# Graph attention with a sort by blocks: smaller first groups, a wide last one, a denser sort plan, and a reordered prologue

## What is computed

```python
q = (x[src] @ qW).reshape(e, 4, 24)
k = (x[dst] @ kW).reshape(e, 4, 24)
v = (x[dst] @ vW).reshape(e, 4, 24)
s = exp(clip(sum(q * k, -1), -10, 10))
w = s / (segment_sum(s, src)[src] + 1e-08)
res = segment_sum(w[:, :, None] * v, src).reshape(6250, 96)
out = layernorm(x + x + res)
```

## Time and profile before

| | us |
|---|---|
| median of 3 runs (lowest, highest) | 1357.38 (1355.97, 1362.27) |
| the profiled execution's own time | 1364.9 |
| its span, first to last instruction | 1363.1 |
| PE busy, share of the span | 1050.7 (77%) |
| DVE busy | 1019.2 (75%) |
| POOL busy | 957.1 (70%) |
| ACT busy | 674.0 (49%) |
| mean granted clock of PE | 0.709 |

### The profile page before, as it was taken

One profiled execution on the slowest core, in us unless ns is written; L12 is line 12 of the kernel. 1 busy time (PEld: TensorE's weight loads), 2 busy tenths in 40 slices (PEclk: granted clock), 3 DMA queues, 4 the chain that ended last, 5 costly groups with the idle time before them and its releaser, 6 DMA issues.

```text
span 1363.1 us, 23400 instructions
## 1 busy us (share of the span) xinstructions
PE 1050.7 (77%) x6502; PEld 935.0 (69%) x6503; DVE 1019.2 (75%) x2846; ACT 674.0 (49%) x1464; POOL 957.1 (70%) x911
## 2 busy tenths in 40 slices
PE   6896498776798786798887778887678888888850
PEld 4674497665787665698776667777577777777740
DVE  8797998689997678998758887777655555555556
ACT  4773299522599522399842225886232222222215
POOL 1203777777787777777777777777777777777745
PEclk9897599956699856599877555889665555555555
DMA  4300222222222222222222222222422222222212
GB/s 121 121 0 25 68 70 70 73 79 70 68 67 69 76 70 73 70 72 72 70 74 79 77 72 74 70 72 82 135 79 78 78 78 78 78 79 78 77 41 71
DMA packets 68298, 100.62 MB, mean 74 GB/s; under 512 B 33522, under 2 KB 53874, under 8 KB 68204
## 3 DMA queue, kind: packets, MB, share of 16 engines
q0 software_dynamic: 42240, 86.56, 23.3%
q1 hardware_dynamic: 25964, 12.94, 3.3%
HBM read 92.23 MB, written 7.22 MB: 73 GB/s over the span
## 4 chain that ended last, share of the span: by engine, by line
POOL 39%; DVE 18%; issue 16%; PE 14%; ACT 7%; DMA 4%; DVEq 2%; POOLq 0%; ACTq 0%; SPq 0%
POOL kv L466 39%; ACT steps_m L672 4%; PE ps_r L620 3%; DMA kv<-kv_table,dst_s 2%; DVE acc L1031 2%; PE ps_q L608 2%; DVE steps_m L800 2%; DVE prod L1039 2%; PE ps_a L594 1%; DVEq L392 1%; PE ps_b L594 1%; DMA acc<-in_x_dram 1%; DVE place_m L940 1%; DVE place_m L944 1%; ACT onehT L717 1%
## 5 line engine op out<-in xcount | busy, mean ns | idle before, releaser
L466 POOL DMA_INDIRECT kv<-kv_table,dst_s x880 | 921.9, 1048 | 329.5 <-issue 322.8
L620 PE MATMUL ps_r<-wv,oneh 128*128 128x100 f32 x1760 | 344.9, 366 | 127.4 <-DVE wv L1046 126.3
L620 PEld LDWEIGHTS ps_r<-wv,oneh 128*128 128x128 f32 x1760 | 312.5, 270 | 150.2 <-DVE wv L1046 141.1
L608 PE MATMUL ps_q<-qt,onehT 128*128 x1760 | 327.3, 353 | 90.9 <-ACT onehT L717 85.9
L608 PEld LDWEIGHTS ps_q<-qt,onehT 128*128 128x128 f32 x1760 | 298.3, 259 | 119.7 <-issue 118.6
L672 ACT ACTIVATE steps_m<-iota_f,pos_t 125x283 f16<-125x283 f32 (+4 forms) x778 | 321.3, 502 | 22.1 <-PE ps_b L594 13.9
L1031 DVE TENSOR_TENSOR acc<-acc,ps_r 128x100 f32 x880 | 223.2, 254 | 65.6 <-issue 32.4
L1039 DVE TENSOR_TENSOR prod<-ps_q,kv 128x480 f32<-128x480 f32 x176 | 115.3, 655 | 208.9 <-DMA kv<-kv_table,dst_s 201.2
L710 ACT ACTIVATE wv<-clipped 128x20 f32<-128x20 f32 x176 | 38.2, 217 | 433.1 <-DVE clipped L1073 432.9
L594 PE MATMUL ps_a<-steps_m,place_m 125*128 125x283 f16 (+4 forms) x778 | 197.8, 294 | 1.7 <-ACT steps_m L672 0.2
L717 ACT ACTIVATE onehT<-ps_t 128x640 f32<-128x640 bf16 x176 | 123.4, 701 | 148.6 <-PE ps_t L629 143.9
(11 more groups left out here) (185 smaller groups left out, 696.4 us busy)
## 6 DMA issues: line engine op xcount, KB each, us to landing
kv<-kv_table,dst_s POOLq DMA_INDIRECT x880
kv_table<-kv SPq DMA_DIRECT2D x7, 672.0 KB, 3.6
acc<-in_x_dram SPq DMA_DIRECT2D x6, 336.0 KB, 4.6
steps_m<-in_x_dram SPq DMA_DIRECT2D x6, 336.0 KB, 5.3
out_dram<-kv SPq DMA_DIRECT2D x6, 336.0 KB
src_i<-in_src_dram SPq DMA_DIRECT2D x1, 415.0 KB
dst_i<-in_dst_dram SPq DMA_DIRECT2D x1, 415.0 KB
acc<-in_x_dram SPq DMA_DIRECT2D x1, 288.0 KB, 5.7
```

The costliest lines, as they stand in the source:

```text
L466: nc.gpsimd.indirect_dma_start(kv[:, nm, u, :], None, kv_dram, bass.IndirectOffsetOnAxis(ap=dst_s[:, n * U + u:n * U + u + 1], axis=0)).th ...
L608: last = nc.tensor.matmul(ps_q[nm % 2][:, u * D:(u + 1) * D], onehT[:, nm % 2, u * P:(u + 1) * P], qt[:, bass.ds(blks[u], 1), :].rearrange ...
L620: last = nc.tensor.matmul(ps_r[nm % 2][:, u * RW:(u + 1) * RW], oneh[:, nm % 2, u, :], wv[:, nm % 2, u, :], start=True, stop=True)
```

## The change

The groups become `[140, 110, 140, 190, 270]` columns, so that `B0 = 0, 17, 39, 66, 103`, still 176 iterations in all, and the steps are 186, 205, 234, 283 and 361 columns wide. The plan of a group now gives its rank steps a computed share of the iterations and spreads the units over the others, up to two in an iteration; one iteration stands ahead of `differ` and `turn` together and one ahead of `pick`, and the first list is written three iterations ahead in place of four. For groups 1 to 4 this makes 7, 9, 11 and 15 rank iterations and 7, 10, 14 and 20 sort iterations. The loops of the main part are written out but for the last stretch. In the prologue `src` comes in two loads, group 0's columns first; x has four buffers in place of two; the first transposes (`lift`) stand behind the marks, projection 0 behind the tally, and the projections 3 to 6 behind `table`. ACT writes the three wide ramps `iota_s`, `iota_d` and `iota_t` in place of DVE, and POOL writes `times_f` and `plus_f`.

```diff
-    LS = 4
+    LS = (3, 4, 4, 4)
     Y = 6
 
-    GC = [180, 150, 170, 190, 160]
+    GC = [140, 110, 140, 190, 270]
...
-    def plan_iters(m, count):
-
-        end = m + count
-        looped = min(max(m, R), end)
-        reps = max(0, min(end, NBT - L) - looped) // R
-        PLAN.append(("iters", m, 0, [None] * (looped - m)))
-        PLAN.append(("loop", looped, reps, 0, 0, (0,) * R))
-        PLAN.append(("iters", looped + reps * R, 0, [None] * (end - looped - reps * R)))
-        return end
-
-    def plan_woven(m, g):
-
-        v, end = V0[g], V0[g + 1]
-        n = max(2, R - m)
-        PLAN.append(("iters", m, g, list(range(v, min(v + n, end + 1)))))
-        m, v = m + min(n, end + 1 - v), v + min(n, end + 1 - v)
-        reps = max(0, end - v) // R
-        PLAN.append(("loop", m, reps, g, v, (1,) * R))
-        m, v = m + reps * R, v + reps * R
-        PLAN.append(("iters", m, g, list(range(v, end + 1))))
-        return m + end + 1 - v
+    def plan_iters(m, count, units=()):
+
+        units = list(units) + [()] * (count - len(units))
+        PLAN.append(("iters", m, 0, units))
+        return m + count
+
+    def plan_last(m):
+
+        looped = max(m, R)
+        PLAN.append(("iters", m, 0, [()] * (looped - m)))
+        reps = max(0, NBT - L - looped) // R
+        PLAN.append(("loop", looped, reps))
+        PLAN.append(("iters", looped + reps * R, 0, [()] * (NBT + 2 - looped - reps * R)))
+
+    def shares(count, parts):
+
+        return [count * k // parts for k in range(parts + 1)]
...
-        project_after = {"mark0": (0,), "count": (1,), "base0": (2, 3), "sel0": (4,), "table": (5, 6)}
+        project_after = {"mark3": ("lift",), f"tally{len(ROUNDS[0]) - 1}": (0,), "count": (1,), "base1": (2,),
+                         "table": (3, 4, 5, 6)}
         for name in rank(0):
             PLAN.append(("piece", name, 0))
             for i in project_after.get(name, ()):
-                PLAN.append(("piece", "project", i))
+                PLAN.append(("piece", "lift", 0) if i == "lift" else ("piece", "project", i))
...
-        for g in range(G - 1):
-
-            end = B0[g + 1] - LS
-            spare = end - 3 - (V0[g + 2] - V0[g + 1] + 1) - m
-            assert spare > 2
-            names = rank(g + 1) + ["choose"]
-            at = 0
-            for k in range(spare):
+        for g in range(1, G):
+
+            end = B0[g] - LS[g - 1]
+            count = end - m - 2
+            names = rank(g) + ["choose"]
+            units = V0[g + 1] - V0[g] + 1
+            ranked = round(count * (12 * GC[g] + 1000) / (34 * GC[g] + 1000))
+            at = shares(len(names), ranked)
+            for k in range(ranked):
                 m = plan_iters(m, 1)
-                to = len(names) * (k + 1) // spare
-                for name in names[at:to]:
-                    PLAN.append(("piece", name, g + 1))
-                at = to
-            m = plan_woven(m, g + 1)
-            for name in ("differ", "turn", "pick"):
-                m = plan_iters(m, 1)
-                PLAN.append(("piece", name, g + 1))
+                for name in names[at[k]:at[k + 1]]:
+                    PLAN.append(("piece", name, g))
+            at = shares(units, count - ranked)
+            PLAN.append(("iters", m, g, [tuple(range(V0[g] + a, V0[g] + b)) for a, b in zip(at, at[1:])]))
+            m = plan_iters(m + count - ranked, 1)
+            PLAN.append(("piece", "differ", g))
+            PLAN.append(("piece", "turn", g))
+            m = plan_iters(m, 1)
+            PLAN.append(("piece", "pick", g))
             assert m == end
-        plan_iters(m, NBT + 2 - m)
+        plan_last(m)
...
-        xc = acc_m[:, 0:2 * CH].rearrange("p (i b d) -> p i b d", i=2, d=D)
+        xc = acc_m[:, 0:4 * CH].rearrange("p (i b d) -> p i b d", i=4, d=D)
...
-            sp.dma_start(src_i[:, :], src.rearrange("(p c) -> p c", c=EC)).then_inc(s_src, 16)
+            src_rows = src.rearrange("(p c) -> p c", c=EC)
+            sp.dma_start(src_i[:, 0:GC[0]], src_rows[:, 0:GC[0]]).then_inc(s_src[0], 16)
             load_x(0, xc[:, 0], s_x[0])
             for i, w in enumerate((qW, kW, vW)):
                 sp.dma_start(w_all[:, i * D:(i + 1) * D], w).then_inc(s_w, 16)
             load_x(1, xc[:, 1], s_x[1])
+            sp.dma_start(src_i[:, GC[0]:EC], src_rows[:, GC[0]:EC]).then_inc(s_src[1], 16)
             sp.dma_start(dst_i[:, :], dst.rearrange("(p c) -> p c", c=EC)).then_inc(s_dst, 16)
 
+            for i in (2, 3):
+                load_x(i, xc[:, i], s_x[i])
...
-                if i + 2 < NPC:
+                if i + 4 < NPC:
                     sp.wait_ge(s_xt, 2 * i + 2)
-                    load_x(i + 2, xc[:, i % 2], s_x[i % 2])
+                    load_x(i + 4, xc[:, i % 4], s_x[i % 4])
...
+            for k, (a, b) in enumerate(((P * 8 - 1, 0), (-P * 8, 1), (-P * 8, 0), (P * 8, 0))):
+                nc.gpsimd.memset(times_f[:, k:k + 1], float(a))
+                last = nc.gpsimd.memset(plus_f[:, k:k + 1], float(b))
+            last.then_inc(s_times, 1)
...
-                if sorts:
-                    unit(*sorts)
+                for sort in sorts:
+                    unit(*sort)
...
+            act.wait_ge(s_ramp, 1)
+            nc.scalar.activation(iota_s[:, :, :], iota_f[:, 0:P].unsqueeze(2).to_broadcast([P, P, SU]), ACT.Copy)
+            nc.scalar.activation(iota_d, iota_f[:, 0:T1].unsqueeze(2).to_broadcast([P, T1, KD]), ACT.Copy)
+            nc.scalar.activation(iota_t[:, :, :], iota_f[:, 1:P + 1].unsqueeze(2).to_broadcast([P, P, U]),
+                                 ACT.Copy).then_inc(s_wide, 1)
...
-            nc.vector.tensor_copy(iota_f[:, :], iota_i[:, :])
+            nc.vector.tensor_copy(iota_f[:, :], iota_i[:, :]).then_inc(s_ramp, 1)
             nc.vector.tensor_copy(iota_u[:, :], iota_i[:, 0:NB])
             link(nc.vector.tensor_copy(part_f[:, :], part_i[:, :]))
-            nc.vector.tensor_copy(iota_t[:, :, :], iota_f[:, 1:P + 1].unsqueeze(2).to_broadcast([P, P, U]))
...
-            link(nc.vector.tensor_copy(iota_s[:, :, :],
-                                       iota_f[:, 0:P].unsqueeze(2).to_broadcast([P, P, SU])))
...
-            link(nc.vector.tensor_copy(iota_d, iota_f[:, 0:T1].unsqueeze(2).to_broadcast([P, T1, KD])))
```

More of the change, by code:

```diff
@@ L271, in gnn @@
         ps_p = ps_r + ps_t
-        s_x = [sem("s_x0"), sem("s_x1")]
+        s_x = [sem(f"s_x{i}") for i in range(4)]
         s_xe = [sem(f"s_xe{i}") for i in range(NPC)]
@@ L280, in gnn @@
         s_w = sem("s_w")
-        s_src = sem("s_src")
+        s_src = [sem("s_src0"), sem("s_src1")]
         s_dst = sem("s_dst")
@@ L284, in gnn @@
         s_const = sem("s_const")
+        s_ramp = sem("s_ramp")
+        s_wide = sem("s_wide")
+        s_times = sem("s_times")
         s_xpad = sem("s_xpad")
@@ L705, in tiles @@
                 if sorts:
-                    unit(*sorts, halves=(0,))
+                    unit(*sorts[0], halves=(0,))
                 n, nm = m, mm
@@ L725, in tiles @@
                 if sorts:
-                    unit(*sorts, halves=(1,))
-            follow(act, tiles, unit, {"project": project, "differ": differ, "turn": turn,
-                                      **{f"tally{r}": lambda g, r=r: tally(g, r) for r in range(len(ROUNDS[G - 1]))}})
+                    unit(*sorts[0], halves=(1,))
+                for sort in sorts[1:]:
+                    unit(*sort)
+            follow(act, tiles, unit, {"lift": copy_xt, "project": project, "differ": differ, "turn": turn,
+                                      **{f"tally{r}": lambda g, r=r: tally(g, r) for r in range(max(len(r) for r in ROUNDS))}})
             act.wait_ge(s_wv, NBT)
@@ L966, in unit @@
             def unit(g, v, vm, between=lambda i: None):
+                if isinstance(v, int) and v == 0:
+                    dve.wait_ge(s_wide, 1)
                 wait(dve, s_bin, v - 1)
@@ L1076, in tiles @@
                 if sorts:
-                    unit(*sorts, between=lambda i: add_up(3 + i))
+                    unit(*sorts[0], between=lambda i: add_up(3 + i))
+                    for sort in sorts[1:]:
+                        unit(*sort)
                 else:
```

40 lines of the change are left out of this document (15 added, 25 removed).

## The result

The changed kernel takes **1406.21 us** (median of 4 runs, 1402.32 to 1407.84) where the kernel before took 1357.62 beside it (4 runs, 1355.97 to 1362.27): 1.034 times as long, 95% interval 1.031 to 1.037. The forecast was 1362 with a range to 1378, so the time lies 44 us above the forecast and outside the range. The profiled execution of the changed kernel took 1402.3 us, with a span of 1400.5.

The account below looks back on a forecast made before the run. POOL's gathers were taken to set the pace. After the change, 97 us to first gather, 759 for four lists, 459 for the last group's gathers and 53 finish gave 1368 us of span, converted to 1362 us; range 1338 to 1378.

Parts of the forecast that it names:

- Ranking: Rank stages of groups 1 to 4, bound by DVE: 39.8 us for 170 columns, 0.11 per column, 3.7 per iteration.
- the term of 759 us: Time for ranking, sorting and closing groups 1 to 4 in turn, against POOL's own 734; fourth list 25 us late.
- Part 2: The gathers: whether the four later groups' lists are ready when POOL, at 6.25 us an iteration, needs them.
- Close of a group: Last sort unit to written list, two iterations lying partly beside its waits: 14 us, 17 for the widest group.
- rival A: The sorters keep up, lists take 734 to 745 us, so time is 1337 to 1348; chance 0.28.
- Start of a sort: Allowance between ranking and sorting in each of groups 1 to 4: 2 us.
- the factor 0.9945: Conversion from profiled run to median time, from the kernel before: 1364.9 profiled, 1357.4 median.
- A wait in one place: POOL idles once, 13 to 37 us, near 830 to 856, for the fourth list; chance 0.59.
- B: PE at low clock bounds group 4's ranking, lists take 774 us, time 1377; chance 0.10.
- C: POOL and DVE hold each other up during gathers, surplus may double, POOL's own 826 us, time 1429; chance 0.03.
- D: Prologue gains less, say dst lands at 16; every case moves up by 3 us; no chance given.
- The break-even: Fourth list must come 754 us after the first gather for no net change; forecast 759.

Follow-up runs that it names:

- The set in between: Changed kernel with groups of 160, 140, 160, 190 and 200 columns, each list four iterations ahead: 1357.06 us, ratio 0.999 to the kernel before.
- control: The changed kernel with nothing edited, run on the chips where the kernel before takes about 1591 us: 1622.48 us, ratio 1.022.

## Why the prediction was wrong

**What held.** The first gather came at 97.91 (forecast 97), PE's first unit at 49.92 (49.6). The rows of the changed kernel:

```profile
14.73 0.23 DVE L812 TENSOR_SCALAR src_i<-src_i 125x140 int32<-125x140 int32 x1 [4.44 <-DMA dst_i<-in_dst_dram]
...
49.92 0.34 PE L597 MATMUL ps_a<-onehT,place_m 125*128 125x186 f16 x1 [2.63 <-ACT steps_m L679]
```

Waiting for `dst` came as said and 1.5 us worse (14.73 for 13.2), and the rest of the prologue made up for it. The tail after the last group's start took 459.4 us (459) and the finish 54.2 (53). Ranking took 305.9 (310.5) and ACT's rate in the sorts was met: 385.8 us busy in the four for 381.6 forecast, 1%. Sum: 97.9 + 789.0 + 459.4 + 54.2 = 1400.5. Three of the four terms are right to 2 us; one is 30 short. That ranking came out so near hides two slips in the working. By its own prices (39.8 for 170 columns, 0.11 a column, 3.7 an iteration) group 1 comes to 51.7 and group 4 to 106.3, where 49.5 and 108.5 stand; they cancel in the sum, and the right ones are nearer to the 51.0 and 105.5 measured.

**What failed** is the term of 759 us: the time of the four lists in Part 2, and in it two prices.

*Close of a group*, forecast 14, 14, 14 and 17, measured 17.8 to 21.5: 78 us for 59, **19 of the 30**. The prediction took the 7.7 us of a close with no iteration inside and let two iterations lie "partly beside its waits". They lie ahead of them. All engines follow one written order, so ACT's copy of the sums and PE's `pick` each queue behind a whole iteration: 4.0 and 4.9 us in the rows of group 1's close, 4 to 5 us for the third iteration in the experiment. 7.7 + 2 × 5 is 17.7, and group 1 measured 17.8. The values of rival A, closes of 11 and 13 us, went the wrong way, and the upper bounds, 17 and for the widest group 20, were under every one measured. The closes that the kernel before has between its iterations, three iterations in each and paced by POOL, lasted 28 to 31 us; the prediction set its price from the one close without iterations and did not bound it by these.

*Start of a sort*, forecast 2 us each: the sorts as a whole took 405.2 for 389.6, 16 over. ACT was idle for 19.5 us in them where the forecast had 8, and 12.9 of these are the two waits at each start, as in the rows at 697.96 to 705.05. The other 4 are the 1% of its busy time. Ranking gave 5 back.

*From span to time.* Of the 44 us, 32.5 are span. The rest is the factor 0.9945: it took the 7.5 us by which one profiled run of before lay above the median of its three runs for a property of the kernel, and the profiled run of after lay 3.9 below its own. Both are differences between single runs.

**A wait in one place** was the wrong picture too, and the prediction had named the waits at groups 1 and 2 as the sign that its stage rates are wrong. The first three lists were judged just in time from margins of 5, 7 and −2 us; stage sums that are 4 to 8% short make each of them late. That did not add to the end, since the chain of lists hardly waits for POOL (4.5 us with a third fewer buffers), but it is why 17 waits for buffers and three for lists came before the fourth list. POOL's own need was over-estimated by 25 us (789.0 less some 80 of waits is 709, forecast 734), without effect, as it was not the longer chain.

**The rivals.** A (the sorters keep up) needed 734 to 746 and got 789. B (PE at the low clock in the big ranking) fell by its own condition: the clock was 0.50 from 610 to 615, where the first tally starts, and 0.99 and 1.00 from 615 to 625, where the second and third run; the ranking took 105.5 us for 108.5. C (the port): the gathers' busy time would have doubled its surplus; it fell by 17.7 us. The Trainium skill, "SBUF — State Buffer", section "SBUF: two separate sides", has the port pair of VectorE and GpSimd as an exclusive lock, for VectorE instructions in a two-port mode or with two SBUF inputs against a GpSimd one that reads SBUF. Longer gathers in the sorts are there in the trace, but mild: 0.13 to 0.26 us over 0.95 each in the four sorts, 0.01 after the last list, and 904.2 us busy in all against 921.9. D: `dst` was late, by a part of its price.

**The range** was too narrow for its sum. The break-even was 5 us away, and 759 was a sum of sixteen stage estimates. 4% on it is 30 us, and the closes' upper bounds alone would have reached only 12.

## What to carry to other kernels

A chain that is hidden by a small margin is priced by its own length, and its short serial steps count most: in a kernel whose engines all follow one written order, each iteration placed ahead of a dependent step costs the chain that iteration's whole time, here 4 to 5 us in the close, whatever idles beside it. Widening the last group so that the prologue gets shorter moves the due time of the last list forward by far more (22 iterations, 137 us of gathers) than the start is gained by (23.5 us). The set in between kept two thirds of that gain, 15.5 us, and had its lists all but in time, yet came out even with the kernel before.

## What the hardware showed that was not expected

Two chips ran the kernel before some 230 us slower than the others, and the rows say why in part. On the first kind of chip the changed kernel's tenth gather ends at 110.4, and DVE takes the second iteration's rows at 112.21. On the second kind, control with six buffers, then eight (each time the last gather before POOL stops for a buffer, the next one, and DVE's product of the second iteration; for the control also that of the first):

```profile
135.74 0.95 POOL L471 DMA_INDIRECT kv<-kv_table,dst_s  x1 [0.30 <-issue]
147.59 0.95 POOL L471 DMA_INDIRECT kv<-kv_table,dst_s  x1 [10.90 <-PE ps_r L623]
```

```profile
107.16 0.66 DVE L1045 TENSOR_TENSOR prod<-ps_q,kv 128x480 f32<-128x480 f32 x1 [0.50 <-DMA kv<-kv_table,dst_s]
...
141.61 0.66 DVE L1045 TENSOR_TENSOR prod<-ps_q,kv 128x480 f32<-128x480 f32 x1 [22.36 <-remote]
```

```profile
149.97 0.94 POOL L471 DMA_INDIRECT kv<-kv_table,dst_s  x1 [0.30 <-issue]
163.65 0.94 POOL L471 DMA_INDIRECT kv<-kv_table,dst_s  x1 [12.73 <-PE ps_r L623]
```

```profile
155.34 0.66 DVE L1045 TENSOR_TENSOR prod<-ps_q,kv 128x480 f32<-128x480 f32 x1 [34.96 <-remote]
```

The tenth gather was issued by 114 in both (111.6 and 113.5). Its landing is seen 30 us later with six buffers, 42 with eight, each time 4 to 5 us after the end of POOL's last issue before its pause. So it looks as if on these chips landings are not seen while GpSimd issues gathers back to back. One row speaks against this in so plain a form: the first five gathers had landed by 107.16, 2.8 us after the fifth was issued, while POOL went on. A plain slower rate does not give the 30 us either: from the last group's start to the last gather (1012.04 to 1569.67, 364 gathers) the control takes 1.53 us a gather, and ten of those would have landed by 115. Eight buffers cost 75 us more than six, and in the two profiles POOL's waits for the four later lists add up to 112.2 us against 43.4. What holds the landings back is open, and four buffers, which this reading says should help there, ran only on the other kind of chip, where they cost 11 and 17 us.

The Trainium skill has two sentences near this. "Perfetto Trace Analysis", section "DMA Instruction — SWDGE (GPSIMD)", says that the profile's end of such an instruction is when GpSimd's last processor has written its descriptors, not when the data has moved; the rows agree, 0.95 us a gather on both kinds of chip. "DMA: Bandwidth & Descriptors", section "Latency and other measured facts", says that DMA engines 7 and 15 are usually slower and guesses that fetching the descriptors that GpSimd writes shares their ports. Whether that is what falls behind here is open; no row shows the DMA engines singly.
